# Four reorderings and a leaner last stage in a fused four-layer kernel

## The chip, the cores and the metric

The kernel runs on one core of a Trainium2 chip. The metric is the device time of one execution in microseconds (us). Engines are TensorE (PE; its weight loads are PEld), VectorE (DVE), ScalarE (ACT), GpSimd (POOL) and SyncE (SP), which only issues transfers here. Ln is line n of the kernel before.

## What is computed

Input u is 8 sequences of 256 tokens with 256 channels. Four residual sublayers follow, each x = layernorm(x + f(x)):

```python
# A: long convolution
q, k = dwconv(u@Wq.T+bq), dwconv(u@Wk.T+bk);  kv = k*(u@Wv.T+bv)
f = ((irfft(rfft(kv)*rfft(ssm)) + kv*D_skip) * q) @ Wo.T + bo
# B: MLP whose gate is changed by attention (16 heads of 16, causal)
x1 = rmsnorm(x)*ln1; mod = 0.1*tanh(attention(x1)@A); h = rmsnorm(x)*ln2
f = x + (silu(h@W_in.T + mod*(h@A)@B) * (h@W_up.T)) @ W_down.T
# D: cumulative sum
f = ((x@Wq.T) * cumsum((x@Wk.T)*(x@Wv.T)) * scale) @ Wo.T
# D: mixture of experts: 64 experts of 176, 6 per token, and a shared expert of 352
w, idx = top_k(softmax(x@gate_w.T), 6);  w = w/sum(w)
f = sum_k w_k * silu(x@w1[idx_k].T)@w2[idx_k].T + (silu(g)*u)@shared_down.T
```

## The kernel before, in words

Everything is f32 apart from masks, one-hot tables and the split parts of q and k. A token tile is 128 tokens, a batch two tiles, the whole 16 tiles.

**Turns.** Batches are pipelined by hand. Turn n works on the long convolution of batch n (parts A and C), attention and MLP of batch n-1 (units u0 to u15, then f0 to f7), cumulative sum, router and shared expert of batch n-2 (D and S), and GpSimd scatters batch n-3 (G). The table ORDER (L327 to L366) lists, for each engine, the order of its parts; each engine issues them in that order and waits on semaphores in between. Turns 0, 1 ("first", "second") and 2 are written out, 3 to 7 are a loop of the list "turn", and two turns empty the pipeline ("last_but_one", "last"). In "last" the last batch is worked on as two halves with the suffixes _0 and _1 (parts E1 to E5 on tiles 14 and 15).

The parts that the change and the steps of the prediction touch:

- *A6, A6o* (DVE, L1547, L1558): mean of squares of the layernormed input of B. Two steps with an accumulated output write squares to xn (L1553) and their mean to ms; L1556 adds epsilon; GpSimd's inverse root (A6n) and A6o follow.
- *D4* (L1074 on PE: transposes of x3 into bank 7; L1317 on ACT: the copy into x3T, L1320). x3 is the input of the experts. *D4l* makes the router's logits, *D4m* their maximum and exponentials, *D4t* and *D4k* the six best and their one-hot sum mkb.
- *S0 to S2*: the shared expert in three parts: matmuls on PE (L1097), tanh on ACT (L1362), two products on DVE (L1818, L1821), which a later part of PE waits for.
- *D5, D5p, D5h* and in the last turn *E5, E5p, E5h*: the rank of a token within its expert (matmuls with a triangular matrix and with seen, the running count), the row that it gets, and the six places per token (L1837, L1739: six masked products, then a reduction). Six scatters per tile on GpSimd (place, L671) write the tokens to x_rows, each for 128 tokens.
- *u0 to u15*: units of attention scores. TensorE makes scores and, three units later, transposes the probabilities, which ACT has exponentiated (L1281), DVE and GpSimd scaled (L640).
- *DTa, DTb* (last turn): from the total of each expert, DTa works out with some thirty small DVE steps which expert and which rows each of 160 chunks of 128 rows has; DTb turns that into one row with four matmuls, and DVE copies it to the table that SyncE reads (L1892). expert_of (L1894) is the same, spread over partitions. idle(n, bank) are matmuls whose result nobody reads.

**Experts.** 40 quads of four chunks. SyncE reads the table and issues for each quad four row loads (L586, 132 KB each) and, where the expert changes, four weight loads (L593, 448 KB each). PE runs with a skew: transposes of quad n (L1161), inner products of quad n-1 (L1172, L1178), outer ones of n-2 (L1189, L1193). ACT has silu (L1375), DVE the copies of transposes (L1913) and results (L1938, in two halves per quad), GpSimd four scatters per quad to y_rows (spread, L705). SyncE's order ahead of the loop is: wait for r_table, weights of quad 0, wait for all scatters (d_scat), rows of quads 0 and 1, weights of quad 1; then rows and weights of quads 2, 3, ...

**Last stage**, 16 token tiles, tile_loop (L435): ACT issues the load of six rows per token (L1388, 768 KB per tile, four buffers), makes five diagonal matrices of the top-k weights (L1396) and issues the output of the tile four before (L1405, 128 KB). PE sums five of the six rows (L1207). DVE does per tile: sixth row plus base (L1952), sum of both (L1955), statistics (L1428), a memset, aggregate (L1432), variance (L1435), and the finish of the tile before (L1440), whose inverse root is GpSimd's (L721). A load waits until the sum L1955 of the tile four before has been made (semaphore f_r).

```python
            def add_last(c):                                   # L1946
                need(dve, "f_out", c.no - 1)
                dve.wait_ge(S[f"f_ld{s}"], c.before(YG) * 16 + 16)
                cf.link(...)                                   # L1952
                dve.wait_ge(S["f_sum"], c.no + 1)
                dve.tensor_tensor(...)                         # L1955
                moments(cf, m, [h]).then_inc(S["n_varF"], 1)
            tile_loop(dve, [add_last, finish])                 # L1965
            tile_loop(act, [collect, None, None, None, put])   # L1412
```

link() waits for the step that it is given; step() only counts it.

## Time and profile before

| | |
|---|---|
| runs shown (3) | 1044.23, 1042.54, 1043.34 us; median 1043.34 |
| profiled execution | 1042.87 us |
| its span (first to last instruction) | 1041.0 us |
| granted clock of TensorE, mean | 0.983 |
| busy: PE, DVE, POOL, ACT | 93%, 60%, 44%, 33% |
| turns | to about 707 us; each of the loop 78.0 to 78.7 us |
| experts | 703 to 979 us |
| last stage | 988 to 1041 us |

The span is what the profiler saw; the time holds 1.87 us more around it. A clock of 1.0 is 2.4 GHz, 0.5 is 1.2 GHz. In rows of a timeline the first number is the start from the span's start, the second the time from the first instruction's start to the last one's end where several are merged (xN), and a bracket tells how long the engine had been idle and what it waited for. Tile names are those of buffers, some of which are used again under other names: w_in, w_up, actT and products hold y rows in the last stage, a_wo and others hold x rows, h1T the scratch of DTa, gs the table, v_sb is xn.

### The profile page before, as it was taken

The numbers are of one execution on the slowest core, as the hardware profiler recorded it, in microseconds if no ns is written. First come the engines' busy times: TensorE is split into PE (matmuls) and PEld (weight loads), VectorE is DVE, ScalarE is ACT, GpSimd is POOL, SyncE is SP. The second block draws the span as 40 slices with busy tenths as digits, with TensorE's granted clock in tenths as the row PEclk, the third lists the DMA queues.
The fourth block names the chain that finished last, engine by engine and source line by source line (L and its number), as shares of the span: only waits on it lengthen the run. The fifth ranks groups of instructions, "written<-read, shape, count | busy, mean of one in ns | idle before, by whom it ended". The sixth has DMA issues, their size and how long they took to land. (4 is left out here: it accounts for less than half of the span.)

```text
span 1041.0 us, 20965 instructions
## 1 busy us (share of the span) xinstructions
PE 973.3 (93%) x6505; PEld 803.4 (77%) x6505; DVE 621.1 (60%) x2090; ACT 338.8 (33%) x1038; POOL 457.1 (44%) x516
## 2 busy tenths in 40 slices
PE   8888999999999999999999899888999999999985
PEld 6766877877877877877877677667888888888874
DVE  4744466676676676666666546663555555555266
ACT  1244263263263263264264262101111111111243
POOL 1142151282283283283283281641566565656621
PEclk9998999999999999999999999898999999999999
DMA  9597790510510510510510510149969697978296
GB/s 364 195 280 121 206 259 8 132 43 17 136 42 16 136 36 21 136 36 21 127 38 22 126 54 11 63 162 347 343 200 345 214 312 229 297 230 302 82 349 215
DMA packets 103271, 163.28 MB, mean 157 GB/s; under 512 B 26961, under 2 KB 77106, under 8 KB 101042
## 3 DMA queue, kind: packets, MB, share of 16 engines
q1 hardware_dynamic: 85746, 113.31, 37.2%
q0 software_dynamic: 12288, 33.96, 8.7%
q10 hardware_dynamic: 5184, 15.36, 4.1%
q8 instruction: 27, 0.44, 0.2%
q14 instruction: 26, 0.21, 0.1%
HBM read 139.32 MB, written 61.87 MB: 193 GB/s over the span
## 5 line engine op out<-in xcount | busy, mean ns | idle before, releaser
L1281 ACT ACTIVATE prob<-bank,nmx 128x128 f32<-128x128 f32 (+1 forms) x256 | 104.8, 431 | 62.0 <-DVE nmx L1585 61.1
L640 POOL TENSOR_TENSOR prob<-prob,rec 128x512 f32<-128x512 f32 x96 | 99.4, 1043 | 41.4 <-DVE rec L1591 40.6
L672 POOL DMA_INDIRECT x_rows<-x_copy,desti x84 | 85.7, 1020 | 18.4 <-issue 18.4
L1585 DVE TENSOR_REDUCE nmx<-bank 128x2 f32<-128x512 f32 (+1 forms) x96 | 65.1, 686 | 46.3 <-PE bank L885 45.7
L1274 ACT ACTIVATE probT<-bank 128x512 f32<-128x512 f32 x96 | 58.0, 604 | 57.0 <-PE bank L745 56.1
L662 POOL TENSOR_TENSOR products<-z,products 128x512 bf16<-128x512 f32 x8 | 9.2, 1156 | 140.6 <-ACT products L1262 140.6
L945 PE MATMUL bank<-h2T,w_up 128*128 128x256 f32 x256 | 66.4, 382 | 0.0
L947 PE MATMUL bank<-h2T,w_in 128*128 128x256 f32 x256 | 65.7, 379 | 0.0
L745 PE MATMUL bank<-cst,prob 128*128 128x128 f32 x384 | 59.6, 279 | 5.2 <-ACT probT L1274 3.6
L1097 PE MATMUL bank<-x3T,sh_gu 128*128 128x256 f32 (+1 forms) x192 | 48.3, 397 | 10.7 <-DVE sact L1821 6.5
L1281 ACT ACTIVATION_READ_ACCUMULATOR prob<-bank,nmx 128x1 f32 x256 | 55.6, 217 | 0.0
L745 PEld LDWEIGHTS bank<-cst,prob 128*128 128x128 f32 x384 | 43.7, 143 | 14.6 <-issue 7.8
L947 PEld LDWEIGHTS bank<-h2T,w_in 128*128 128x128 f32 x256 | 48.7, 190 | 6.6
L945 PEld LDWEIGHTS bank<-h2T,w_up 128*128 128x128 f32 x256 | 45.0, 191 | 8.6
L1938 DVE COPY d_kv<-bank 128x512 f32<-128x512 f32 x20 | 13.8, 691 | 60.7 <-PE bank L1193 60.7
L1097 PEld LDWEIGHTS bank<-x3T,sh_gu 128*128 128x128 f32 (+1 forms) x192 | 33.9, 185 | 20.8 <-DVE sact L1821 8.8
L958 PE MATMUL bank<-w_down,actT 128*128 128x256 f32 x224 | 49.5, 379 | 0.0
L1375 ACT ACTIVATE kc<-bank 128x384 f32<-128x384 f32 x20 | 9.8, 490 | 120.4 <-PE bank L1178 120.4
L1303 ACT ACTIVATE gt<-bank 128x256 f32<-128x256 f32 x64 | 24.4, 383 | 74.9 <-PE bank L950 69.7
L1938 DVE COPY d_wq<-bank 128x512 f32<-128x512 f32 x20 | 13.8, 691 | 57.8 <-PE bank L1193 57.8
L1375 ACT ACTIVATE x<-bank 128x384 f32<-128x384 f32 x20 | 9.8, 491 | 117.8 <-PE bank L1178 117.8
L304 POOL TENSOR_TENSOR spare<-ones_row 128x1 f32<-128x1 f32 x49 | 9.2, 189 | 88.1 <-DVE d_cs L1938 56.6
(442 smaller groups left out, 2526.9 us busy)
## 6 DMA issues: line engine op xcount, KB each, us to landing
w_in<-in_e_w SPq DMA_DIRECT2D x20, 448.0 KB
w_up<-in_e_w SPq DMA_DIRECT2D x20, 448.0 KB
w_down<-in_e_w SPq DMA_DIRECT2D x20, 448.0 KB
products<-in_e_w SPq DMA_DIRECT2D x20, 448.0 KB
prob<-in_e_w SPq DMA_DIRECT2D x20, 448.0 KB
probT<-in_e_w SPq DMA_DIRECT2D x20, 448.0 KB
actT<-in_e_w SPq DMA_DIRECT2D x20, 448.0 KB
x_rows<-sgt SPq DMA_DIRECT2D x1, 8320.0 KB, 28.9
```

Of the source, the lines that this page charges most:

```text
L640: pool.tensor_tensor(p, p, r, ALU.mult).then_inc(S["b_scaled"], 1)
L672: pool.indirect_dma_start(x_rows, bass.IndirectOffsetOnAxis(ap=desti[:, n:n + 1].bitcast(U32), axis=0), rows[:, n // TOPK, :], None).then_ ...
L745: return pe.transpose(out, x, ident)
L945: pe.matmul(psum(n, L, 2 * L), w_up[:, kt, cols], h2T[:, kt, :], start=(kt == 0), stop=(kt == KT - 1))
L947: pe.matmul(psum(n, 0, L), w_in[:, kt, cols], h2T[:, kt, :], start=(kt == 0), stop=False)
L958: mm = pe.matmul(psum(1, tt * D, (tt + 1) * D), actT[:, f, tt * P:(tt + 1) * P], w_down[:, f, :], start=(f == 0), stop=(f == FT - 1))
L1097: mm = pe.matmul(bank[0:w, spread_of(b, n), g * L:(g + 1) * L], sh_gu[:, kt, g * SH_I + at:g * SH_I + at + w], x3T[:, kt, :], start=(kt == ...
L1274: act.activation(probT[:, turned % PROBTS, :, :], bank[:, 2, :].rearrange("p (j q) -> p j q", j=4), ACT.Copy).then_inc(S["b_pT_out"], 1)
L1281: i = act.activation(prob[:, u % PROBS, h * w:(h + 1) * w], psum(u % 2, h * w, (h + 1) * w), ACT.Exp, bias=nmx[:, u, h:h + 1], accum_out=s ...
L1303: act.activation(gt[:, f % 2, :], psum((0, 2, 3)[f % 3], 0, L), ACT.Tanh, scale=0.5).then_inc(S["b_gt"], 1)
L1585: dve.tensor_reduce(nmx[:, u, 0:512 // w], bank[:, u % 2, :].rearrange("p (h k) -> p h k", k=w), AX, ALU.max, negate=True).then_inc(S["b_m ...
L1938: dve.tensor_copy(yc[s], bank[:, to:to + 2, 0:D]).then_inc(S["m_y_out"], 1)
```

## The change

- A6 writes the squares to PSUM bank 5, and the step that adds epsilon takes the larger of (mean + epsilon) and the first square of that bank, which is never the larger one.
- In the list "turn" ACT's D4 moves from behind u9 to ahead of it.
- D5h and E5h: the six products accumulate into destf; the reduction goes.
- List "last": PE has E3_1 ahead of E4l_0, S2 behind E5_1, no DTa, 5 idle matmuls for 9 in DTb; E5_1 makes the totals with three more matmuls, and seen is no longer updated there. DVE has E3n_1 ahead of E4m_0, both selections ahead of the places E5h_0, and the places E5h_1 behind DTa and DTb; the copy of expert_of is a part of its own, DTe, behind them. The table is copied in two halves, experts first, each with an increment of r_table.
- SyncE issues the weights of quads 0 and 1 after the first half, then waits for the second and for d_scat, then issues the rows.
- spread: in quads 38 and 39 the first two scatters wait for the first half of the result only.
- Last stage: collect moves from ACT to SyncE. DVE's steps are five parts of three tiles, in this order: sum of tile n-1, finish of n-2, statistics of n-1, sixth row of n, aggregate and variance of n-1.

```diff
-"act": "... u8 u9 D4 u10 S0 ..."                                (turn)
+"act": "... u8 D4 u9 u10 S0 ..."
-"pe": "... E3_0 E2x_1 E2q_1 E4_0 E4l_0 E3_1 E4_1 E4l_1 E5_0 S0 S1 S2 E5_1 DTa DTb SDa SDb"   (last)
+"pe": "... E3_0 E2x_1 E2q_1 E4_0 E3_1 E4l_0 E4_1 E4l_1 E5_0 S0 S1 E5_1 S2 DTb SDa SDb"
-"dve": "... E4m_0 E3n_1 E4t_0 E3o_1 E4k_0 E4m_1 E5p_0 E4t_1 E5h_0 E4k_1 E5p_1 E5h_1 DTa DTb S0 S1 S2 D4w SD"
+"dve": "... E3n_1 E4m_0 E3o_1 E4t_0 E4k_0 E4m_1 E5p_0 E4t_1 E4k_1 E5h_0 E5p_1 DTa DTb E5h_1 DTe S0 S1 S2 D4w SD"
@@ sync
-            load_weights(Quad(0, 0))
+            for n in range(2):
+                load_weights(Quad(0, n))
+            sp.wait_ge(S["r_table"], 2)
             sp.wait_ge(S["d_scat"], 16 * TT * TOPK * NB)
             for n in range(2):
                 load_rows(Quad(0, n))
-            load_weights(Quad(0, 1))
             quad_loop(sp, [load], begin=2)
+            def collect(c):
+                s = c.slot(YG)
+                if first(c.no):
+                    sp.wait_ge(S["m_y"], 2 * QUADS)
+                need(sp, "f_r", c.no - (YG - 1))
+                rows = ...
+                sp.dma_start(yg[s], y_rows[rows, :].rearrange(...)).then_inc(S[f"f_ld{s}"], 16)
+            for s in range(4):
+                sp.wait_ge(S[f"m_st{s}"], 32 * (QUADS // 2))
+            tile_loop(sp, [collect])
@@ gpsimd, spread
-                pool.wait_ge(S["m_y_out"], 2 * c.no + 2)
+                late = isinstance(c.no, int) and c.no >= QUADS - 2
+                pool.wait_ge(S["m_y_out"], 2 * c.no + (1 if late else 2))
                 alone(pool)
                 for k in range(4):
+                    if late and k == 2:
+                        pool.wait_ge(S["m_y_out"], 2 * c.no + 2)
@@ tensor, E5
+                    if tt:
+                        pe.matmul(tot, onesb, mkb[:, 0, :], start=True, stop=False)
+                        pe.matmul(tot, onesb, mkb[:, 1, :], start=False, stop=False)
+                        pe.matmul(tot, onesb, seen[:], start=False, stop=True)
@@ scalar
-            tile_loop(act, [collect, None, None, None, put])
+            tile_loop(act, [ahead, None, None, None, put])
@@ vector, A6
-                    i = dve.scalar_tensor_tensor(xn[:, tt, :], slot(b, tt), 1.0 / D, slot(b, tt), ALU.mult, ALU.mult, accum_out=...)
+                    i = dve.scalar_tensor_tensor(psum(5, tt * D, (tt + 1) * D), slot(b, tt), 1.0 / D, slot(b, tt), ALU.mult, ALU.mult, accum_out=...)
-                dve.tensor_scalar(nrm["R"]["v"][:], ms[:], RMS_EPS, None, ALU.add).then_inc(S["n_varR"], 1)
+                dve.scalar_tensor_tensor(nrm["R"]["v"][:], ms[:], RMS_EPS, psum3(5)[:, :, 0], ALU.add, ALU.max).then_inc(S["n_varR"], 1)
@@ vector, E5p and E5h (D5h alike)
-                    if tt == TT - 1:
-                        for n in range(TT):
-                            cd.link(dve.tensor_tensor(seen[:], seen[:], mkb[:, n, :], ALU.add))
-                        i = dve.scalar_tensor_tensor(hit[:, tt, k, :], ..., ALU.is_equal, ALU.mult)
-                    cd.link(i)
-                    cd.step(dve.tensor_reduce(destf[:, tt, :], hit[:, tt], AX, ALU.add))
+                        i = dve.scalar_tensor_tensor(hit[:, tt, k, :], ..., ALU.is_equal, ALU.mult, accum_out=destf[:, tt, k:k + 1])
+                    cd.step(i)
@@ vector, DTa and DTb
-                dve.wait_ge(S["r_tot"], 1)
+                dve.wait_ge(S["d_rank"], b + TT)
-                dve.tensor_copy(table, bank[0:1, 0, :]).then_inc(S["r_table"], 1)
+                for k in range(2):
+                    dve.tensor_copy(table[:, k * 2 * P:(k + 1) * 2 * P], bank[0:1, 0, k * 2 * P:(k + 1) * 2 * P]).then_inc(S["r_table"], 1)
@@ vector, last stage
-            tile_loop(dve, [add_last, finish])
+            tile_loop(dve, [(1, add_sum), (2, finish), (1, spread_of_rows), (0, add_last), (1, variance)])
```

## Rows read from the trace of the kernel before

**Rows 1.** Waits of TensorE in one turn, 476 to 555 (us, times, longest)
```profile
PE bank L1097 <- DVE sact L1821: 1.1, 1, 1.1
...
PE bank L1097 <- ACT x3T L1320: 0.6, 1, 0.6
```

**Rows 2.** Timeline of that turn (start us, us, engine line op, idle before)
```profile
552.87 1.56 DVE L1556 TENSOR_SCALAR vR<-ms 128x2 f32<-128x2 f32 x1
...
553.35 1.05 POOL L640 TENSOR_TENSOR prob<-prob,rec 128x512 f32<-128x512 f32 x1
...
554.79 0.42 DVE L1821 SCALAR_TENSOR_TENSOR sact<-sgs,bank 128x256 f32<-128x256 f32 x1
...
555.26 1.97 PE L1097 MATMUL bank<-x3T,sh_gu 128*96 128x256 f32 x8 [1.11 <-DVE sact L1821]
```

**Rows 3.** All instances of line L1556 (durations ns min/median/max)
```profile
L1556 DVE TENSOR_SCALAR vR<-ms x8: 168/1554/1558, 35.5 to 552.9; 128x2 f32<-128x2 f32 x8
```

**Rows 4.** Timeline of the same turn, 541 to 553
```profile
546.61 0.60 ACT L1320 ACTIVATE x3T<-bank 128x512 f32<-128x512 f32 x1
...
548.63 2.03 POOL L640 TENSOR_TENSOR prob<-prob,rec 128x512 f32<-128x512 f32 x2
```

**Rows 5.** Timeline of the last turn, 655 to 694
```profile
675.03 6.62 PE L1097 MATMUL bank<-x3T,sh_gu 128*128 128x256 f32 x24
...
677.86 0.55 DVE L1741 TENSOR_REDUCE destf<-sact 128x6 f32<-128x384 f32 x1
...
685.77 0.22 DVE L1860 TENSOR_SCALAR h1T<-bank 128x64 f32<-128x64 f32 x1 [1.21 <-PE bank L1129]
...
692.04 0.68 DVE L1892 CAST gs<-bank 1x512 int32<-1x512 f32 x1 [0.73 <-PE bank L1136]
```

**Rows 6.** Chain that ended last: scatter, row load, quad 2
```profile
693.15 4.44 DMA x_rows<-x_row,desti
...
707.36 5.04 DMA a_wo<-x_rows
...
712.45 1.97 PE bank L745 x8
```

**Rows 7.** Chain that ended last: scatters of y_rows
```profile
976.39 0.98 POOL y_rows L713
...
985.38 2.40 DMA y_rows<-d_wk,ids
```

**Rows 8.** Chain that ended last: inner products of quads 1, 2 and 3
```profile
714.42 3.41 PE bank L1172 x16
...
723.02 1.79 PE bank L1172 x16
...
729.69 1.79 PE bank L1172 x16
```

**Rows 9.** Stretches: us; PE, PEld, DVE, ACT, POOL busy; PEclk, DMA share, GB/s
```profile
714.00:716.00 2.00, 2.00 (x11) 2.00 (x11) 1.80 (x14) 0.00 (x0) 0.00 (x0) 0.50 1.03 408
...
992.00:996.00 4.00, 3.77 (x17) 3.34 (x18) 1.61 (x7) 0.14 (x1) 0.00 (x0) 1.00 1.02 426
...
1000.00:1004.00 4.00, 3.29 (x16) 2.55 (x14) 3.25 (x13) 2.95 (x10) 1.30 (x2) 1.00 0.97 276
...
1012.00:1016.00 4.00, 3.79 (x18) 3.00 (x18) 3.07 (x12) 2.50 (x9) 0.69 (x1) 1.00 0.98 346
```

**Rows 10.** Timeline of the last stage, 994 to 1037
```profile
994.76 0.42 DVE L1955 TENSOR_TENSOR qc<-qc,bank 128x256 f32<-128x256 f32 x1 [2.07 <-PE bank L1207]
...
995.22 0.43 DVE L1428 BATCH_NORM_STATS2 stF<-qc 128x6 f32<-128x256 f32 x1
...
1034.38 0.42 DVE L1955 TENSOR_TENSOR qc<-qc,bank 128x256 f32<-128x256 f32 x1
...
1035.52 0.15 DVE L1435 TENSOR_SCALAR vF<-mvF 128x1 f32<-128x1 f32 x1
...
1036.47 0.41 DVE L1440 TENSOR_SCALAR w_up<-qc,mvF,yF 128x256 f32<-128x256 f32 x1 [0.43 <-POOL yF L721]
```

More of the change, by code:

```diff
@@ L435, in tile_loop @@
         def tile_loop(eng, skewed):
+            lags = skewed if isinstance(skewed[0], tuple) else list(enumerate(skewed))
             def step(i, off):
-                for lag, work in enumerate(skewed):
+                for lag, work in lags:
                     c = Tile(i, off - lag)
@@ L446, in tile_loop @@
                     step(i, off)
-            for off in range(NT, NT + len(skewed) - 1):
+            for off in range(NT, NT + max(lag for lag, _ in lags)):
                 step(0, off)
@@ L603, in _ @@
                 load_rows(Quad(0, n))
-            load_weights(Quad(0, 1))
             quad_loop(sp, [load], begin=2)
+            def collect(c):
[3 more added lines that the diff above has]
+                need(sp, "f_r", c.no - (YG - 1))
+                rows = (slice(c.no * P * TOPK, (c.no + 1) * P * TOPK) if isinstance(c.no, int)
+                        else bass.ds(c.no * P * TOPK, P * TOPK))
+                sp.dma_start(yg[s], y_rows[rows, :].rearrange("(p k) d -> p k d", k=TOPK)).then_inc(S[f"f_ld{s}"], 16)
+            for s in range(4):
+                sp.wait_ge(S[f"m_st{s}"], 32 * (QUADS // 2))
+            tile_loop(sp, [collect])
         @block.gpsimd
@@ L1122, in shared_out @@
                 return part
-            def DTa(b):
-                idle(9, 3)
-                pe.wait_ge(S["d_pos"], b + TT)
-                pe.wait_ge(S["d_dest"], b + TT)
-                pe.matmul(psum(6, 0, E_N), onesb, seen[:], start=True, stop=True).then_inc(S["r_tot"], 1)
             def DTb(b):
-                idle(9, 3)
+                idle(5, 3)
                 pe.wait_ge(S["r_tab"], 1)
@@ L1378, in _, with ahead @@
             quad_loop(act, [None, silu])
-            def collect(c):
-                s = c.slot(YG)
-                if first(c.no):
-                    act.wait_ge(S["m_y"], 2 * QUADS)
+            def ahead(c):
                 need(act, "f_r", c.no - (YG - 1))
-                rows = (slice(c.no * P * TOPK, (c.no + 1) * P * TOPK) if isinstance(c.no, int)
-                        else bass.ds(c.no * P * TOPK, P * TOPK))
-                act.dma_start(yg[s], y_rows[rows, :].rearrange("(p k) d -> p k d", k=TOPK)).then_inc(S[f"f_ld{s}"], 16)
                 if not isinstance(c.no, int):
@@ L1836, in D5h @@
                     for k in range(TOPK):
[L1837 to L1839 removed]
+                        i = dve.scalar_tensor_tensor(hit[:, tt, k, :], iota, idxf[:, tt, k:k + 1], pos[:, tt, :], ALU.is_equal, ALU.mult,
+                                                     accum_out=destf[:, tt, k:k + 1])
+                cd.step(i)
                 need(dve, "d_copied", b)
@@ L1903, in _ @@
                         **{f"S{n}": shared(n) for n in range(3)}, "SD": SD})
-            for ch, more in ((ca, 0), (cbn, 2), (cd, 14)):
+            for ch, more in ((ca, 0), (cbn, 2), (cd, 11)):
                 assert ch.k == ch.per + more, (ch.name, ch.k, ch.per)
@@ L1947, in add_last, with add_sum, spread_of_rows, variance @@
                 h, s = c.slot(2), c.slot(YG)
-                cf.start(c.no)
                 need(dve, "f_out", c.no - 1)
                 dve.wait_ge(S[f"f_ld{s}"], c.before(YG) * 16 + 16)
-                cf.link(dve.scalar_tensor_tensor(m["r"][:, h, :], yg[s][:, ON_PE, :], tile_of(TOPW, c.no)[:, ON_PE:TOPK],
-                                                 tile_of(X, c.no), ALU.mult, ALU.add))
+                dve.scalar_tensor_tensor(m["r"][:, h, :], yg[s][:, ON_PE, :], tile_of(TOPW, c.no)[:, ON_PE:TOPK],
+                                         tile_of(X, c.no), ALU.mult, ALU.add).then_inc(S["f_part"], 1)
+            def add_sum(c):
+                h, s = c.slot(2), c.slot(YG)
+                dve.wait_ge(S["f_part"], c.no + 1)
                 dve.wait_ge(S["f_sum"], c.no + 1)
                 dve.tensor_tensor(m["r"][:, h, :], m["r"][:, h, :], psum(s, 0, D), ALU.add).then_inc(S["f_r"], 1)
+            def spread_of_rows(c):
+                h = c.slot(2)
                 dve.wait_ge(S["f_r"], c.no + 1)
-                moments(cf, m, [h]).then_inc(S["n_varF"], 1)
+                cf.start(c.no)
+                cf.step(dve.bn_stats(m["st"][:, h, :], m["r"][:, h, :]))
+            def variance(c):
+                h = c.slot(2)
+                cf.start(c.no, 1)
+                cf.wait()
+                alone(dve)
+                cf.link(dve.bn_aggr(m["mv"][:, h, :], m["st"][:, h, :]))
+                dve.tensor_scalar(m["v"][:, h:h + 1], m["mv"][:, h:h + 1, 1], LN_EPS, None, ALU.add).then_inc(S["n_varF"], 1)
             def finish(c):
```

29 lines of the change are left out of this document (13 added, 16 removed), and 4 rows, old and new, of the table ORDER.

## The prediction

> **What bounds the kernel now.** I read the chain that ended last first, then what TensorE waits for in one turn of the loop, then the timelines of the four places that the change touches. The chain is TensorE nearly throughout: the seven turns of attention and MLP, then 40 quads of experts at 6.67 us each, then a last stage of 16 token tiles. Work leaves the path only where TensorE waits. In one turn (78.3 us) those waits are few: 1.1 us before the third part of the shared expert, 0.6 us before its first part, 0.7 us elsewhere [rows 1]. So VectorE, ScalarE and GpSimd count only where such a wait ends on them.
>
> The first wait: VectorE's two-column step that adds epsilon (L1556) takes 1.56 us, and ends when GpSimd's product of probabilities ends (554.40); the shared expert's gate waits behind it, its result is there at 555.21, and TensorE, free since 554.15, starts at 555.26 [rows 2]. The step took 0.17 us where GpSimd left it alone and 1.55 in the middle of eight [rows 3]; it is long in five turns, 3 to 7.
>
> The second wait: x3T's copy stands on ScalarE behind the exponentials of unit 9 and starts at 546.61 [rows 4], though its input was there at 544.42.
>
> **The change, part by part**, against the profiled execution: 1042.87 us, of which the span is 1041.0; the median of the runs shown is 0.47 us above it.
>
> *Squares in PSUM.* The squares go to bank 5 and the epsilon step reads a PSUM column; the maximum changes no value. It has then one SBUF operand, as L1821 has, which runs in 0.42 us for 256 columns beside GpSimd's work [rows 2]. Bounds for the step: 0.17 us, as when left alone [rows 3], and the 1.56 of today. I take 0.2. Then the gate is free to start when ScalarE's tanh ends, 0.9 us sooner; TensorE's wait of 1.11 falls to 0.2, as the tanh itself follows its matmuls. What follows in the turn hangs on these matmuls and moves with them; the next GpSimd product is ready at about 556.2, when TensorE needs it. 5 turns x 0.9 = 4.5 us. The Trainium skill (SBUF — State Buffer, "SBUF: two separate sides") says that VectorE steps in a two-port mode, or with two SBUF inputs against a GpSimd step that reads SBUF, and GpSimd exclude each other for a whole instruction; the trace agrees for L1556. The same rule speaks against counting the squares as free: they keep two SBUF inputs, and would gain nothing where GpSimd is at work.
>
> *x3T ahead of exponentials.* The copy starts at about 544.8, in a gap of 0.40 us that ScalarE has there, so the exponentials lose 0.1 at most. TensorE's 0.64 us wait goes in six turns. But what comes next is late: after this part TensorE transposes unit 8, which GpSimd scales from 548.63 for 1.0 us [rows 4], behind two scatters and the inverse root, none of which waits for x3T. In turns 3 to 7 the wait moves there: gain 0. In turn 2, without scatters, half remains: 0.3 us. Bounds: 0 and 6 x 0.64 = 3.8.
>
> *Places without a reduction.* The accumulator replaces one VectorE step (0.55 us for six columns [rows 5]) and a link, per half. In the turns this stands in the MLP, where TensorE never waits for VectorE: 0. Running totals of tile 15 come from three more small matmuls instead of two additions and TensorE's separate sum.
>
> *Table ahead of last places.* Today rank 1 is ready at 681.7, behind 24 shared matmuls (675.03 to 681.65); the table's arithmetic starts at 685.77, its row is copied at 692.04 [rows 5]. After: the last eight of the 24 stand behind rank 1, the shared matmuls start somewhat sooner, and the arithmetic starts at about 680.0 without the round trip over TensorE. Table row: 680.0 + 6.27 = 686.3. Weights of quads 0 and 1 are then issued at 687 to 693, beside the scatters. The price: the places of tile 15 follow the table, 686.3 + 0.7 (two half copies for one of 0.68) + 1.7 (today's places less the reduction) = 688.7. The first six scatters end at about 687, so GpSimd waits 1.8 us and the last scatter starts at 695.2 instead of 693.15 [rows 6]: worse by 2.0. It landed after 4.44 us with weights in flight; GpSimd's last scatter of y_rows, alone, took 2.40 [rows 7]. I take 3.3, landed at 698.5 against 697.59, bounds 697.6 and 699.7.
>
> From there SyncE needs 9.77 us to the last row load of quad 2, of which 2.9 (702.4 to 705.3) are the weights of quad 1 that now lie before: last issue at 705.4 instead of 707.36. It landed in 5.04 us; quad 1's rows, with little beside them, in about 2.8 (issued 702.0, used 704.8). So the rows lie at 708.2 to 710.4 instead of 712.40 [rows 6]. Before that, TensorE must take quad 1's rows (landed 705.7) and quad 0's inner products: 3.9 us today (704.84 to 708.74), 6.7 at half clock (712.45 to 719.16, today's first after the wait). I take 711.5 for quad 2's start (709.6 to 712.4) against 712.45: 0.9 us. And the clock: today TensorE waits 3.9 us at that point, then runs at a granted 0.5 (1.2 GHz) [rows 9], and the 16 matmuls L1172 take 3.41 us against 1.79 at 2.4 GHz; from quad 2's start to the next inner products are 10.57 us, where the later pattern gives 6.67 for a quad and 0.87 for the transposes [rows 8]. Without that wait the 3.0 us go; a part may return in quads 0 and 1, which is why I took 711.5. Sum 3.9 us, bounds 0.5 (cold in both places) and 5.9.
>
> *Later scatters of y.* In quad 38 GpSimd needs one half of the result only. It starts at 976.39 today after waiting for the second [rows 7], though it is free at 974.96. It then starts 1.0 us sooner, and the eight scatters are back to back: 1.0 us, bounds 0.7 and 1.1.
>
> *Last stage.* Today a step is (1034.38 - 994.76)/15 = 2.64 us [rows 10]. Three rates lie near it. TensorE: 3.79 us busy for 18 matmuls at ten a tile, 2.1 us [rows 9]. DMA: 768 KB in and 128 KB out per tile, 917 kB; at 426 GB/s (the stretch 992 to 996) 2.15 us, at 346 (1012 to 1016) 2.65 [rows 9]. VectorE: the new order hides the half-microsecond of links, but finishing tile n-1 now waits in line for its root: variance to finish is 0.95 us (1035.52 to 1036.47) [rows 10], and finish (0.41), statistics (0.43), part sum (some 0.48) and aggregate (0.2) follow, with some overlap: 2.3 to 2.45. Loads: a buffer's cycle today includes ScalarE's waits for the output before it; on SyncE the load follows the sum at once, some 1.8 us sooner. That fills the hole after 1000, where only 276 GB/s flowed [rows 9]; with more loads waiting, near 390 GB/s is plausible, 2.35 us. I take 2.42: 15 x 0.22 = 3.3 us. The tail grows: after the last sum the order puts another finish ahead of the statistics, 2.8 us to the last finish instead of 2.09: -0.7. Net 2.6, bounds 0 and 5. SyncE has nothing else queued then, and waits only for the same results as ScalarE did.
>
> Sum: 4.5 + 0.3 + 3.9 + 1.0 + 2.6 = 12.3 us. 1042.87 - 12.3 = 1030.6; for the median, 1031.0.
>
> **Rivals.**
> 1. *DMA holds the last stage.* Rates near 346 GB/s lasted while VectorE had work; the engines were busy all the time there. Then the step stays 2.65, with the tail 0.7 longer: that part gives -0.8, total 8.9, time 1034.4. For it: busy share about 1.0 in both stretches. Against: the same share carried 426 GB/s. The Trainium skill (DMA: Bandwidth & Descriptors, "Specifications") gives some 358 GB/s per core as the memory's limit; by that figure a step would be no less than 2.56 us (an estimate from the page), between this rival and my sum. The 426 GB/s of this trace are above it.
> 2. *The late places eat the middle.* GpSimd waits in front of the seventh scatter, TensorE stands idle longer before quad 0 and runs quads 0 and 1, even 2, at half clock: middle +0.5 instead of 3.9, time 1034.4. For it: TensorE slowed at once after a wait of 3.9 us. Against: rows arrive in three steps now, with work between.
> 3. *x3T's gain stays.* If the POOL chain were bound by TensorE after all, five turns give 0.6 each: 3 us more, 1028.
> 4. *The epsilon step still waits*, or something takes its place before the third shared part: 4.5 lost, 1035.5. L1821's 0.42 us speaks against.
> 5. *Slower.* Loads on SyncE's queue and outputs on ScalarE's share the engines with less order, and the rate stays below that of the worst stretch of this stage, some 250 GB/s against 276 [rows 9]: 3.67 us a step for 917 kB. Then the stage costs 15 x 1.03 + 0.7 = 16.2 us more and takes all 9.7 us of the rest: 1049.8. It turns the sign from a step of 3.25 us on. For it: rates this low occur; against: they occur where few loads are out.
>
> **How the numbers follow.** Chances: forecast 0.48, rival 1 0.15, rival 2 0.13, rival 3 0.08, rival 4 0.10, rival 5 0.04, and 0.02 for about no change. About 0.2%, 2.1 us, is what a measurement of this kernel can tell. Rivals 1 to 4 are all faster than that, singly; two or three together reach 1038 to 1041, so I shift 0.02 to "same". Range: down to 1027.5 (rival 3, or a good last stage), up to 1037.5 (two of 1, 2, 4 together).
>
> **What would show it.** L1556's successor at 0.2 us and the wait before the third shared part near 0.2 in turns 3 to 7; no wait for x3T, but one for GpSimd's product right behind. Table row near 686, last x scatter near 695, quad 2's start near 711 at full clock. First y scatter of quad 38 within 0.5 us of the one before. Steps of 2.4 us in the last stage. Wrong would be: turns still 78.3 us, quad 2 after 713, or steps of 2.6.

## The result, and the profile after

The changed kernel takes 1038.92 us (median of 20 runs, 1036.81 to 1044.68), the kernel before, on the same chip, 1043.02 (20 runs). The ratio is 0.9972, 95% interval 0.9961 to 0.9983: faster by 0.28%, 4.1 us less instead of the 12.3 of the forecast, and outside its range. The profiled execution took 1040.91 us (span 1038.8), against 1042.87 (span 1041.0).

| start of (us in the profile) | before | after | moved | forecast |
|---|---|---|---|---|
| last x3T copy of the turns' form | 618.65 | 613.86 | -4.8 | -4.8 |
| silu of quad 5 | 745.5 | 740.9 | -4.6 | -8.7 |
| first sum of the last stage | 994.76 | 989.26 | -5.5 | -9.7 |
| last sum | 1034.38 | 1032.07 | -2.3 | -13.0 |
| end of the span | 1041.0 | 1038.8 | -2.2 | -12.3 |

So the turns came out as forecast, the middle brought nothing, the later scatters their 0.9, and from the first to the last sum the kernel lost 3.2 us where 3.3 were to be won. What follows the last sum grew by 0.1 us, not by 0.7. Of the 4.8 us of the turns, four turns of the loop brought 4.1 (78.51 us each before, 77.49 after), the stretch before them 1.1, and the turn behind them gave back 0.4. The loop starts anywhere from 230.6 to 234.1 us in the runs of kernels that are alike up to there, so it is partly luck that the sum meets the forecast to 0.1 us.

One turn of the changed kernel, 471 to 549: TensorE's waits (us, times, longest), and every instance of the new epsilon step (durations in ns). They answer to [rows 1, 3].

```profile
PE bank L764 <- POOL prob L656: 1.0, 1, 1.0
PE bank L826 <- ACT kvT L1257: 0.4, 1, 0.4
PE bank L764 <- ACT probT L1290: 0.3, 1, 0.3
```
```profile
L1565 DVE SCALAR_TENSOR_TENSOR vR<-ms,bank x8: 156/156/157, 35.7 to 549.3; 128x2 f32<-128x2 f32 x8
```

The waits for sact and for x3T are gone, and the second has turned into one for GpSimd's product.

The middle, from the chain that ended last (against [rows 6]), with two stretches of the windows view (columns as in [rows 9]), and TensorE's longest wait there, from 690 to 730. The second row of the chain is the last row load of quad 3.

```profile
691.24 5.79 DMA x_rows<-x_row,desti
...
709.82 6.35 DMA tabA<-x_rows
```
```profile
698.00:702.00 4.00, 0.47 (x2) 0.48 (x3) 0.00 (x0) 0.00 (x0) 0.00 (x0) 0.54 0.74 195
702.00:706.00 4.00, 3.65 (x22) 3.25 (x21) 2.39 (x4) 0.00 (x0) 0.00 (x0) 0.61 0.86 215
```
```profile
PE bank L764 <- DMA v<-x_rows: 5.6, 1, 5.6
```

Before, TensorE's waits from 700 to 735 were these:

```profile
PE bank L745 <- DMA a_wo<-x_rows: 3.7, 1, 3.7
...
PE bank L745 <- DMA v<-x_rows: 0.5, 1, 0.5
```

The last scatter starts 1.9 us earlier than before, yet 2.9 later counted from the x3T copy, and takes 5.79 us to land among the weights of two quads (4.44 before, 3.3 forecast). Then SyncE issues twelve row loads in a row, 132 KB each 0.52 us, and the DMA engines carry only 195 to 215 GB/s.

TensorE's wait has moved: the 3.7 us in front of quad 2 (rows of a_wo) are gone, and 5.6 us stand in front of quad 0 (rows of v), where 0.5 stood. Its granted clock is 0.54 and 0.61 from 698 to 706, and 1.00 from there on. The rows of quad 2 are taken at 708.29, which is 94.4 us after the last x3T copy against 93.8 before (712.45). Thanks to the full clock quad 2's silu comes 0.9 us sooner by that count, but quad 5's 0.2 later: TensorE waits 1.0, 0.4 and 0.2 us for rows of later quads, where it had no such wait before.

The last stage: VectorE's waits for outputs (us, times, longest), the landing of outputs (L1415; before: 1.7/3.3/5.1), and the timeline around the longest wait.

```profile
DVE w_in L1448 <- DMA out<-w_in: 5.7, 4, 3.2
DVE w_up L1448 <- DMA out<-w_up: 5.4, 4, 2.3
```
```profile
DMA to landing us min/median/max: 1.7/5.1/6.9
```
```profile
1010.27 0.34 ACTq L1415 DMA_DIRECT2D out<-w_in  x1
...
1013.38 0.42 DVE L1967 TENSOR_TENSOR qc<-qc,bank 128x256 f32<-128x256 f32 x1
...
1014.00 0.33 SPq L617 DMA_DIRECT2D w_up<-y_rows  x1
1017.00 0.41 DVE L1448 TENSOR_SCALAR w_in<-qc,mvF,yF 128x256 f32<-128x256 f32 x1 [3.19 <-DMA out<-w_in]
...
1018.46 0.42 DVE L1967 TENSOR_TENSOR qc<-qc,bank 128x256 f32<-128x256 f32 x1
1019.07 0.33 SPq L617 DMA_DIRECT2D actT<-y_rows  x1
```

There are two output buffers, w_in and w_up. The finish of a tile (L1448) stands in VectorE's line ahead of the next sum (L1967), and it can't write before the output of two tiles ago has landed: issued at 1010.27, it was there at 1017.0. The next sum comes 5.08 us after the last, and the load that waits for that sum as late (1014.00, then 1019.07). In all there are 11.1 us of such waits; the kernel before had none.

### The profile page after: what moved, and what is told of

Same layout as the page of the kernel before. It is cut to its first block and busy times, and to the rows that moved or that the text cites. A ratio compares the mean times of both kernels' runs of the same rounds, so it can differ in the third digit from the quotient of the medians.

```text
span 1038.8 us, 21002 instructions
## 1 busy us (share of the span) xinstructions
PE 970.8 (93%) x6481; PEld 800.4 (77%) x6481; DVE 605.5 (58%) x2176; ACT 339.0 (33%) x1038; POOL 454.5 (44%) x516
## 5 line engine op out<-in xcount | busy, mean ns | idle before, releaser
L656 POOL TENSOR_TENSOR prob<-prob,rec 128x512 f32<-128x512 f32 x96 | 99.2, 1041 | 40.7 <-DVE rec L1600 39.8
L977 PEld LDWEIGHTS bank<-w_down,actT 128*128 128x128 f32 x224 | 42.5, 190 | 5.9
```

Of the source, the lines that this page charges most:

```text
L656: pool.tensor_tensor(p, p, r, ALU.mult).then_inc(S["b_scaled"], 1)
L977: mm = pe.matmul(psum(1, tt * D, (tt + 1) * D), actT[:, f, tt * P:(tt + 1) * P], w_down[:, f, :], start=(f == 0), stop=(f == FT - 1))
```

## The experiments

There were eighteen runs of fourteen kernels, on five chips. On four of them (e1 to e4, e5 to e8, e13 to e16, e17 and e18) the kernel before took 1091.6 to 1100.7 us, on the fifth (e9 to e12) 1042.1. The turns of the changed kernel take the same time on all (77.6 us in e2 as in e11). The difference lies in the part after them, where on the four chips the trace shows engine waits that end on nothing it knows (in e2 110 us of ScalarE's and 70 of VectorE's, in e11 none). I therefore compare ratios within one chip, and stretches of the traces. "G" below is the changed kernel with four output buffers. D is the start of a thing in us, counted from the last-but-one turn's copy x3T, and "step" is the time from the first to the last sum of the last stage, divided by 15.

**The last stage.**

e1_last_old puts the old stage back:

```diff
-            tile_loop(dve, [(1, add_sum), (2, finish), (1, spread_of_rows), (0, add_last), (1, variance)])
+            tile_loop(dve, [add_last, finish])
-            tile_loop(sp, [collect])
-            tile_loop(act, [ahead, None, None, None, put])
+            tile_loop(act, [collect, None, None, None, put])
```


> The changed kernel with the last stage of before (ScalarE issues the loads, VectorE's old order); everything else stays changed. My theory: the changed last stage lost time, because the finish of a tile waits for its output buffer (11.1 us in all) and holds the next sum and with it the next load; 3.3 us from the first landed load to the end against before. With the old stage the step is 2.64 us again (2.85 in the changed kernel), no wait for an output over 0.3 us, and the time 3 us under the changed kernel's 1038.9: about 1036. Rival (the last stage is innocent, its start merely drifted): 1038.9, step 2.6 or more.

e2_out4 (G):

```diff
-                need(dve, f"f_st{h}", c.before(2) * 16)
-                scaled(m, {h: outb[h]}).then_inc(S["f_out"], 1)
+                dve.wait_ge(S[f"f_st{c.slot(YG)}"], c.before(YG) * 16 + 1)
+                scaled(m, {h: outb[c.slot(YG)]}).then_inc(S["f_out"], 1)
```

(put takes slot(YG) too, and each of the four semaphores starts at 1.)

> The changed kernel with four output buffers in the last stage instead of two. Theory (two buffers are the cause): VectorE's waits for an output fall from 11.1 us to under 1, the step from 2.85 to 2.4 to 2.5, the time from 1038.9 to 1033 (1031.5 to 1035). Rival (the DMA rate itself is the limit, the wait for outputs only shows it): the same time is then spent in waits for loads, the step stays 2.75 to 2.85, the time within 1 us of 1038.9.

e3_loads_act moves only `collect` back to ScalarE:

> The changed kernel with the loads of the last stage issued by ScalarE again, as before; VectorE keeps the new order. Theory (outputs land late because loads on another queue are ahead of them): outputs land in a median of about 3.3 us as before (5.1 in the changed kernel), the waits for outputs fall under 3 us in all, the step is 2.5, the time 1034 to 1036. Rival (the new order of VectorE alone makes the waits, wherever loads come from): waits for outputs stay near 11 us, step 2.8, time 1038 to 1039.

e4_dve_old takes back only VectorE's order:

> The changed kernel with VectorE's old order in the last stage (sixth row, sum, statistics, variance of a tile, then the finish of the tile before); SyncE keeps the loads. Theory: the outputs still land late (median near 5 us) and the finish, now last in the step, still holds the next sum; step 2.7 to 2.85, time 1037.5 to 1039.5. Rival (new order is the culprit): the step is 2.5 or less and the time under 1035.5.

Measured, with the ratio to the kernel before on that chip (1091.57 us):

| | ratio (interval) | first to last sum, us | step | waits for outputs | outputs land, median |
|---|---|---|---|---|---|
| before (first chip) | 1 | 39.62 | 2.64 | 0 | 3.3 |
| changed (first chip) | 0.9972 | 42.81 | 2.85 | 11.1 | 5.1 |
| e1 old stage | 0.9930 (0.9897 to 0.9963) | 40.36 | 2.69 | 0 | 3.3 |
| e2 four buffers | 0.9875 (0.9817 to 0.9934) | 35.94 | 2.40 | 0 | 5.7 |
| e3 loads on ScalarE | 0.9896 (0.9860 to 0.9931) | 37.60 | 2.51 | 0.8 | 3.9 |
| e4 old VectorE order | 0.9951 (0.9913 to 0.9990) | 40.96 | 2.73 | 2.1 | 4.3 |

Each step came as the theory said (e1's fits its rival too, which had "2.6 or more"), and the rivals' of e2, e3 and e4 did not. Four buffers alone turn 2.85 into 2.40, though outputs land even later. Against the old stage (e1, 2.69) the new order alone is worth 0.2 us a step (e3, 2.51), loads on SyncE alone about nothing (e4, 2.73); only both together, with two buffers, give the 2.85. The changed kernel itself did not run on this chip; on the fifth chip it did, and has 2.89 (e11, below). VectorE's wait for the sum in e2 (us, times, longest), the whole stretch from the first to the last sum, one part of it, and these two sums:

```profile
DVE qc L1970 <- PE bank L1223: 11.2, 16, 2.4
```
```profile
1025.43:1061.37 35.94, 33.51 (x150) 27.26 (x148) 26.43 (x104) 18.84 (x60) 7.89 (x15) 1.00 0.90 333
...
1038.00:1042.00 4.00, 3.74 (x18) 2.91 (x17) 2.23 (x9) 2.44 (x9) 1.08 (x2) 1.00 1.04 420
```
```profile
1025.43 0.42 DVE L1970 TENSOR_TENSOR qc<-qc,bank 128x256 f32<-128x256 f32 x1 [2.41 <-PE bank L1223]
...
1061.37 0.42 DVE L1970 TENSOR_TENSOR qc<-qc,bank 128x256 f32<-128x256 f32 x1 [0.38 <-PE bank L1223]
```

In its last stage VectorE waits for little but TensorE now (0.7 us for an inverse root), and TensorE is busy for 33.5 of 35.9 us. The absolute times missed their expectations, because they had been given for the first chip.

**The middle.** e5_mid_old is G with the last turn as before (lists, totals, table in one piece, weights of quad 1 behind the rows); the places still accumulate.

> The kernel with four output buffers, and in the last turn everything as before: the old lists, TensorE's separate total, table in one piece behind the places, weights of quad 1 behind the rows. Squares in PSUM, x3T, late scatters and the new last stage stay. Theory (the middle brought next to nothing, because what the table gained was given back to the scatter and to loads): ScalarE's copy x3T of tile 15 at 668.8 (667.4 in the changed kernel), quad 2's silu about 1 us later than in the changed kernel (720.6), quad 4's within 0.5 us of its 733.7. Rival (the middle's 3.9 us are there and something else lost them): quad 4's silu at 736 or later.

e6_w1_late and e7_places_early undo a part each:

```diff
 e6:
-            for n in range(2):
-                load_weights(Quad(0, n))
+            load_weights(Quad(0, 0))
...
             for n in range(2):
                 load_rows(Quad(0, n))
+            load_weights(Quad(0, 1))
 e7:
-"... E5h_0 E5p_1 DTa DTb E5h_1 DTe S0 ..."
+"... E5h_0 E5p_1 E5h_1 DTa DTb DTe S0 ..."
```


> The kernel with four output buffers; SyncE issues the weights of quad 1 behind the rows of quads 0 and 1 again, the table stays ahead of the last places. Theory (weights beside the scatter made it land late: 5.79 us against 4.44): the last scatter of x, started at about 691.2, lands within 4.6 us, the first row load is issued at about 695.9 instead of 697.6; but the last row load of quad 2 is issued 9.8 us after the landing instead of 6.9, at about 705.6 instead of 703.9, so quads 2 to 4 are no earlier, rather up to 1.3 us later. Rival (the weights of quad 1 play no part in the scatter's landing): it lands 5.5 us or more after its start.

> The kernel with four output buffers; VectorE makes the places of tile 15 ahead of the table again (the two selections, the new totals and the split copy stay). Theory (the late places delay the scatters, and the last scatter is what the rows wait for): the last scatter starts at about 689.2 instead of 691.2 and lands 1.5 to 2 us sooner, the table is copied 2 us later (684.7), and quad 2's silu is up to 1.5 us sooner than 719.7. Rival (the loads of the early quads are held by the DMA rate, near 400 GB/s from 710 on): the first two quads move, but quad 4's silu stays at 733.7, within 0.5 us.

| D of | table | last x scatter | first row load | quad 2 | quad 5 | ratio |
|---|---|---|---|---|---|---|
| e2 (G) | 66.7 | 75.6 | 81.9 | 106.1 | 130.0 | 0.9875 |
| e5 old middle | 79.5 | 73.8 | 84.0 | 111.9 | 136.8 | 0.9951 |
| e6 weights of quad 1 late | 66.9 | 75.8 | 81.4 | 107.5 | 132.4 | 0.9890 |
| e7 places early | 69.7 | 73.7 | 80.9 | 107.2 | 132.1 | 0.9905 |
| e8 (G's middle, see below) | 67.6 | 76.5 | 83.0 | 106.4 | 131.3 | 0.9886 |

e2 ran on another chip than the other four, so e8, which has G's middle, is their neighbour. In all runs with the new middle where the kernel before takes 1091 us or more, quad 5 lies between 129.5 and 133.3 (e1 to e4, e8, e14, e18), and with the old middle between 135.5 and 137.1 (e5, e13, e16, e17). So on these chips the rival wins: the old middle is 6.8 us slower than in e2 and 5.5 slower than in e8. Its table is 12 to 13 us later, where 4.9 lie between the two on the first chip (73.4 and 68.5), and its first row load has to wait for the table and the weights of quad 0 behind it. That this is the whole loss is not shown. VectorE stands still ahead of the table's arithmetic until 685.16, though TensorE's total was there at 681.5 (the timeline of e17_mid_old_3, the same kernel):

```profile
685.16 0.23 DVE L1871 TENSOR_SCALAR h1T<-bank 128x64 f32<-128x64 f32 x1 [5.31 <-remote]
```

"remote" is a releaser that the profile doesn't know; what it is stays open. e6's scatter landed after 5.08 us, between both expectations. In e7 the scatter started 1.9 us sooner than in e2, but the rows only 1.0: SyncE was still issuing weights. Neither undone part is seen to give anything back: quad 5 is at 132.4 and 132.1, inside the spread of 129.5 to 133.3 that the new middle has by itself. These two runs can't tell an effect of 2 us or less.

e8_eps_old is G with the old step, `dve.tensor_scalar(nrm["R"]["v"][:], ms[:], RMS_EPS, None, ALU.add)`, the squares staying in PSUM.

> The kernel with four output buffers; the squares still go to PSUM, but epsilon is added by the old two-column step, which reads and writes SBUF alone. Theory (the step waits because of its own form, wherever the squares go): it takes 1.5 us again in turns 3 to 7, and x3T of the last-but-one turn starts at 618.6 instead of 613.9, so 4 to 5 us later: 0.4% more time than the kernel with four output buffers. Rival (what helped is that the squares left SBUF): the step takes 0.2 us, and the turns stay at 77.5 us.

Neither theory held. Ratio 0.9886 (0.9842 to 0.9931), the step and its instances (ns):

```profile
L1565 DVE TENSOR_SCALAR vR<-ms x8: 169/170/1466, 36.5 to 550.3; 128x2 f32<-128x2 f32 x8
```

Seven are short and the last is long, with the same operands. The timeline shows why:

```profile
472.76 0.17 DVE L1565 TENSOR_SCALAR vR<-ms 128x2 f32<-128x2 f32 x1
473.51 1.05 POOL L656 TENSOR_TENSOR prob<-prob,rec 128x512 f32<-128x512 f32 x1
...
550.27 1.47 DVE L1565 TENSOR_SCALAR vR<-ms 128x2 f32<-128x2 f32 x1
...
550.65 1.05 POOL L656 TENSOR_TENSOR prob<-prob,rec 128x512 f32<-128x512 f32 x1
```

Where the step starts 0.75 us ahead of GpSimd's product, it gets through. Where it starts 0.38 us ahead, it is held until the product ends (0.48 in [rows 2]). This kernel also has the new place of x3T, so the suspicion fell on that edit.

**The turn, one edit at a time**, each on the kernel before. e9_x3t_alone has only `u8 D4 u9` for `u8 u9 D4` in ScalarE's list; e10_squares_alone only the two lines of A6; e11_after_again is the changed kernel beside them; e12_w2_first is G with one more move:

```diff
-            for n in range(2):
-                load_rows(Quad(0, n))
-            quad_loop(sp, [load], begin=2)
+            load_rows(Quad(0, 0))
+            load_weights(Quad(0, 2))
+            for n in range(1, 3):
+                load_rows(Quad(0, n))
+            quad_loop(sp, [load], begin=3)
```


> The kernel before with one edit: in the list of the loop's turn ScalarE's copy x3T stands ahead of the exponentials of unit 9. My prediction's theory: TensorE's wait moves to GpSimd's product, the old epsilon step still takes 1.55 us in turns 3 to 7, turns stay at 78.5 us, time unchanged (within 0.5 us). Second theory, from the run that kept the old step behind squares in PSUM (0.17 us in turns 3 to 6): the copy's new place moves the moment at which the step comes, so it falls outside GpSimd's product; then it takes 0.17 us in most turns with the squares still in SBUF, the turn is 77.6 us, the time 3 to 4.5 us less (0.3 to 0.4%).

> The kernel before with one edit: squares in PSUM and the epsilon step with the larger-of operand from PSUM. My prediction's theory: the step takes 0.2 us in all turns and the turn falls from 78.5 to 77.6 us, time 4 to 4.5 us less (0.4%). Second theory (either edit alone lets the step through, or each takes half): with the copy x3T in its old place the step is short, but TensorE's next wait, for GpSimd's product, keeps part of it: turn 77.9 to 78.3 us, time 1 to 3 us less.

> The changed kernel itself, as the measure for the runs beside it. No theory is told apart by it alone; it gives the place of its last sum and its last-stage step (2.85 us in its first profile) beside those of the kernel with four output buffers (2.40). If the two output buffers are the cause, its waits for outputs are again about 10 us and its step over 2.7.

> The kernel with four output buffers, and SyncE issues the weights of quad 2 between the rows of quad 0 and those of quad 1. Theory (the early quads are bound by the DMA rate, and the hole of some 200 GB/s that twelve row loads in a row leave from 698 to 706 gave back what the early weights had won): the hole is filled to 350 GB/s or more, and quads 4 and 5 start their silu 1 to 3 us sooner than in the kernel with four output buffers, while quad 1 starts up to 2.5 us later. Rival (the rows are what TensorE waits for): quads 1 to 5 all start 2 to 2.6 us later.

The kernel before took 1042.12 us here (35 runs):

| | us | ratio (interval) | last-but-one x3T | D first row load | D quad 5 | step |
|---|---|---|---|---|---|---|
| before (first chip) | 1043.02 | 1 | 618.65 | 79.4 | 126.8 | 2.64 |
| e9 x3T alone | 1038.74 | 0.9972 (0.9959 to 0.9986) | 614.7 | 78.0 | 125.2 | 2.66 |
| e10 squares alone | 1037.95 | 0.9974 (0.9960 to 0.9987) | 614.7 | 79.1 | 124.4 | 2.59 |
| e11 changed kernel | 1042.81 | 0.9997 (0.9981 to 1.0013) | 613.2 | 83.9 | 126.3 | 2.89 |
| e12 weights of quad 2 | 1039.61 | 0.9975 (0.9956 to 0.9994) | 616.3 | 82.2 | 131.6 | 2.45 |

e9, all instances of the old step with the squares still in SBUF, and the turn's end:

```profile
L1556 DVE TENSOR_SCALAR vR<-ms x8: 168/169/170, 35.5 to 548.5; 128x2 f32<-128x2 f32 x8
```
```profile
548.55 0.17 DVE L1556 TENSOR_SCALAR vR<-ms 128x2 f32<-128x2 f32 x1
...
549.37 1.05 POOL L640 TENSOR_TENSOR prob<-prob,rec 128x512 f32<-128x512 f32 x1
```

and e10, where the same closeness as before does no harm to the step with a PSUM operand:

```profile
550.32 0.16 DVE L1556 SCALAR_TENSOR_TENSOR vR<-ms,bank 128x2 f32<-128x2 f32 x1
550.69 1.05 POOL L640 TENSOR_TENSOR prob<-prob,rec 128x512 f32<-128x512 f32 x1
```

For x3T the second theory holds, mine fell (gain 0.3 forecast, 3.9 in the trace); for the squares mine stood (4.5 and 3.9). The length of a turn says it best, as the place of the copy also holds where the loop starts: the mean of four turns is 78.51 us before, 77.56 in e9, 77.64 in e10 and 77.53 in e11. So either edit alone gives nearly all, 0.9 us a turn, since both cure one wait, and both together 1.0. And either alone makes a kernel no slower than the whole change: e11 is 4.1 and 4.9 us above them by the medians (2.6 and 2.4 by the ratios, whose intervals overlap a little), so on this chip the rest of the change costs what the turns bring, and the changed kernel is no faster than the one before. In e11 the waits for outputs are 12.1 us, as expected. The last stage takes 43.4 us from first to last sum there and 39.95 in e9: 3.4 us. The middle is the rest: quad 5 is 1.1 us later in e11 than in e9 and 1.9 later than in e10, by D.

Both have the old middle, and yet TensorE's 3.7 us in front of quad 2 have shrunk by themselves, to 1.4 us in e9 and 2.2 in e10. In their place 3.2 and 2.3 us stand in front of quad 0's rows, where 0.5 stood. Up to quad 2 TensorE waits no less (5.1 and 4.9 us, 4.8 before), but its clock is 1.00 when it takes quad 2's rows (0.50 before, [rows 9]), and quad 2's silu comes 3.0 and 3.4 us sooner by D. In e9 the scatter landed in 3.31 us, against 4.44 before with the weights issued equally close behind it (waits of TensorE, 696 to 760, and the chain):

```profile
PE bank L745 <- DMA v<-x_rows: 3.2, 1, 3.2
PE bank L745 <- DMA a_wo<-x_rows: 1.7, 2, 1.4
```
```profile
688.93 3.31 DMA x_rows<-x_row,desti
...
702.84 5.44 DMA a_wo<-x_rows
708.33 1.09 PE bank L745 x8
```

e12 went as its rival said, only worse. The hole was filled (369 GB/s at 706 to 710), but quad 1's rows lay behind the weights, and TensorE waited for rows 5.4 and 7.4 us at half clock:

```profile
PE bank L766 <- DMA ssm<-x_rows: 7.4, 1, 7.4
PE bank L766 <- DMA v<-x_rows: 5.4, 1, 5.4
```
```profile
706.00:710.00 4.00, 0.00 (x0) 0.00 (x0) 0.00 (x0) 0.00 (x0) 0.00 (x0) 0.50 1.04 369
```

That cost 5.3 us by D of quad 5, and yet e12 is 3.2 us under the changed kernel beside it: its last stage has the step of 2.45. So the cure by four buffers holds on this chip too (2.89 in e11).

**Repeats.** e13 is e5's kernel and e14 e2's, e15_places_w1 undoes e6's and e7's parts together, e16_turns is the kernel before with both edits of the turn; e17 and e18 are e13 and e14 again. All fell on chips where the kernel before takes 1098.6 to 1100.7 us.

> The kernel of e5_mid_old again (four output buffers, last turn as before), now beside the kernel it is compared with. Theory (the new middle costs time: the places late, and the last scatter landing among the weights of two quads): the last scatter of x lands 77.5 to 79 us after the last-but-one turn's copy x3T instead of 83, quad 5's silu comes 124.5 to 125.5 us after it instead of 126.5 to 127, and the time is 1.5 to 2.5 us under that of e14_out4_2: about 1032.5 where the kernel before takes 1042. Rival (the middle is neutral): both within 0.7 us of each other.

> The kernel of e2_out4 again (the changed kernel with four output buffers). Theory: VectorE's waits for outputs are gone, the step of the last stage is 2.40 to 2.45 us instead of 2.85, and the time is 1034 to 1035.5 where the kernel before takes 1042 and the changed kernel 1039 to 1042. Rival (the DMA rate holds the stage on this chip too): 1038 or more.

> The kernel with four output buffers, the places of tile 15 ahead of the table as before, and the weights of quad 1 behind the rows as before; totals over PSUM without TensorE's separate sum, both selections ahead of the places of tile 14 and the split copy stay. Theory (late places and early weights are the whole cost of the new middle): the last scatter starts about 74 us after the last-but-one turn's copy x3T and lands by 78; time as e13_mid_old_2 or up to 1 us less, since the table is sooner by TensorE's round trip. Rival (something else in the new lists costs): it stays with e14_out4_2, 1034 or more.

> The kernel before with the two edits of the turn, squares in PSUM and the copy x3T ahead of unit 9's exponentials; middle and last stage as before. Theory (the two overlap, and the rest of the change costs more than it brings): 4.7 us less than before, 0.5 of it beyond either edit alone: 1037 to 1037.5 where the kernel before takes 1042, and thus 1.5 us or more under the changed kernel. Rival (the two add up): 1034.

> The kernel of e5_mid_old once more. On chips where the kernel before takes 1042 us: row loads start 78 to 79.5 us after the last-but-one turn's copy x3T (83.8 in the changed kernel), quad 5's silu 124.5 to 126 us after it (126.3 to 127.0 in the changed kernel), time 1032 to 1033.5. On chips where the kernel before takes some 1095: the table comes at 78 to 79.5 us, quad 5 at 136, as in e5_mid_old and e13_mid_old_2. Rival (the middle is neutral where code is fetched without stalls): within 0.7 us of e18_out4_3 there.

> The kernel of e2_out4 once more, the changed kernel with four output buffers. On chips where the kernel before takes 1042 us: step of the last stage 2.40 to 2.45 us, time 1034 to 1036, 4 to 6 us under the changed kernel; quad 5 at 126.3 to 127.0. On chips where the kernel before takes some 1095: 1.1 to 1.3% under it, as in e2_out4 and e14_out4_2.

| | ratio (interval) | D quad 5 | step |
|---|---|---|---|
| e13 old middle | 0.9944 (0.9906 to 0.9983) | 135.5 | 2.36 |
| e14 G | 0.9888 (0.9849 to 0.9928) | 131.1 | 2.33 |
| e15 | 0.9914 (0.9875 to 0.9954) | 133.1 | 2.36 |
| e16 both edits of the turn | 0.9889 (0.9837 to 0.9941) | 137.1 | 2.66 |
| e17 old middle | 0.9892 (0.9816 to 0.9968) | 136.9 | 2.36 |
| e18 G | 0.9862 (0.9822 to 0.9901) | 133.2 | 2.52 |

G is 1.1 to 1.4% under the kernel before in three runs there, and its step lies between 2.33 and 2.52 in all. On these chips the new middle helps in every pair: quad 5 is 6.8, 4.4 and 3.7 us sooner with it (e5 and e2, e13 and e14, e17 and e18), and e15 lies between. e13's theory, by which the new middle costs time, fell here, though only by D: the intervals of the ratios overlap in each pair. What e17 and e18 expected for such chips came about. e16's interval is too wide to say what the second edit of the turn adds, and its profiled execution (1098.76 us) was nearly the longest of its six. **Open** stays whether, where the kernel before takes 1042 us, the old middle beats the new with all else equal, and what G takes there: neither kernel came to such a chip. G ought to be near e12 less what its middle lost, 1039.6 - 5.3 = 1034.3 us; that is worked out, not measured.

## Why the prediction was wrong, point by point

- **The last stage (2.6 us forecast, 3.3 lost).** The failed step is the sum of VectorE's steps, "2.3 to 2.45", with "on SyncE the load follows the sum at once". It counts the finish among the steps and leaves out what the finish waits for. Before, it found its buffer free, as an output lands in 3.3 us and the finish comes late in the step. With the loads on a queue of their own the outputs landed in 5.1, and the new order put the finish ahead of the sum on which the next load hangs. e2 shows that this alone was the loss: with four buffers the step is 2.40 (2.45 in e12, beside the changed kernel's 2.89). That it meets the 2.42 of the forecast is partly luck. The forecast had VectorE and the transfers as limits and TensorE at 2.1 us a tile; in e2 TensorE is busy for 33.5 us in 15 steps, 2.23 each, and VectorE waits for it. The tail was mis-sized too: the last finish comes 2.15 us after the last sum (1034.22 less 1032.07), not 2.8. Rival 1 named the wrong cause (engines full at 346 GB/s): e2 has 420 GB/s in one stretch. By the figure of the Trainium skill that the prediction names (DMA: Bandwidth & Descriptors, "Specifications"), some 358 GB/s, a step could not be under 2.56 us (an estimate from it). The step alone does not speak against it, since four of the sixteen loads are out before the first sum, and e2 moved 333 GB/s on the mean between the sums; this also makes the 917 kB a step of the prediction too much. But the 420 GB/s here and the 426 of [rows 9] are above the figure, so the measurement decides. Rival 5 had the queues in it, but as a rate, not as a wait.
- **The middle (3.9 forecast, nothing got on the first chip).** Two terms failed. The first is the landing of the last scatter, and with it the rows. The forecast had the last scatter landed 0.9 us later than before, counted from the x3T copy; it was 4.2. Of the 3.3 in excess the start made 0.8 (77.4 us after the copy, 76.6 forecast), and the landing 2.5: "I take 3.3", it was 5.79, and the bound named was 4.44, the number of before. In the ten traces with both quads' weights issued ahead of it and a landing in the chain it took 5.67 us or more, in e6, with one quad's, 5.08, and in e15, with half of these, 4.38. That the weights are the cause fits this, but is not shown: in e9 and before, with the same order, it took 3.31 and 4.44. TensorE then stood 5.6 us before quad 0's rows, at a clock that fell to half. That is what rival 2 described. The second term is the base: the wait of TensorE and its half clock in front of quad 2 were taken as a property of the old order. Both single-edit kernels have that order and full clock there, with quad 2's silu 3.0 and 3.4 us sooner by D. The full clock from 706 on came as forecast. Where the gain at quad 2 goes by quad 5 is seen in part only (waits of 1.0, 0.4 and 0.2 us for rows); the rest stays open.
- **The turns (4.8 forecast, 4.8 got).** Right as a sum, wrong in the parts. The step that failed is that x3T brings 0.3: only what TensorE waits for next was followed, not that everything behind moves some 0.3 us against GpSimd's product. Whether the step of [rows 2] is held depends on that: 0.48 us ahead was too late, 0.75 early enough. The squares' 0.9 a turn held up (e10, 0.87), though L1821, taken as its pattern, ran when the product had ended (554.79 against 554.40); e10 is what shows it. The Trainium skill (SBUF — State Buffer, "SBUF: two separate sides") has the exclusion per instruction; the traces agree, and add that it is a matter of phase. By the profile the step that is held starts first, 0.38 to 0.48 us before the product.
- **The later scatters (1.0 forecast).** 0.9: from quad 39's silu to the first sum it was 23.31 us before and 22.40 after.
- **The chances.** Two terms failed together. The text had this (two or three rivals at once, 1038 to 1041) but gave it 2 in 100, as if the terms failed independently and seldom. The upper end of the range does not follow from its own working either: two of the rivals 1, 2 and 4 together give 1037.8 to 1038.9 us, not 1037.5.

## What to carry to other kernels

When a step is moved up in an engine's line, list what it waits for, its output buffer too, and who now stands behind that wait; a transfer's landing time is not a constant but was longer in these runs when another queue had loads in flight. A wait of one engine for another's instruction to end is cured as well by shifting the phase as by changing operands: try edits singly before adding their gains. A stall that the trace of one execution shows at a seam between stages may be chance of phase; look whether it survives an unrelated edit before counting it as something to win, and when it is gone, look where TensorE waits instead.

## What the runs showed of the hardware that was not expected

- An output of 128 KB landed in a median of 3.3 us with loads on the same queue, 5.1 and 4.3 with them on another queue (changed kernel, e11), and 5.4 to 6.5 in the kernels with four output buffers, whose steps are shorter (5.7 in e2). The Trainium skill (DMA: Bandwidth & Descriptors, "Queues, rings and completion order") says that each engine takes turns between queues; no run here shows the turns themselves.
- The last x scatter landed in 4.44 and 3.31 us with the weights of quad 0 issued right behind it (before, e9), in 5.08 with these issued ahead of it (e6) and 4.38 with half of them (e15), and in 5.67 to 6.86 with two quads' weights ahead (changed kernel, e1 to e4, e8, e11, e12, e14, e18).
- The same program took 1042 us on one chip and 1092 to 1101 on four others, with waits that have no releaser, as the 5.31 us above, in the parts behind the turns. There the edit of the middle that brought nothing on the first chip was worth 3.7 to 6.8 us by D of quad 5.
